# Graph layer kernel: where ScalarE copies a pair's sums out of their bank in the joint part

## The reference

```python
h = jnp.maximum(_layernorm(x, axis=-1), 0.0)             # x: 50000 x 256
S = h[src]                                                # 50000 edges
for r in range(2):                                        # edge type picks the weights
    msgs = where(rel == r, relu(relu(S @ W.T + b) @ W.T + b), msgs)
agg = segment_sum(msgs, dst, num_segments=50000)
i, f, g, o = split(agg @ W_ih.T + b_ih + b_hh, 4)
c = sigmoid(i) * tanh(g);  hn = sigmoid(o) * tanh(c)
y = relu(hn @ W1.T + b1);  y = relu(y @ W2.T + b2)
return x + y @ W3.T + b3
```

## Time and profile before

| | |
|---|---|
| median of 3 runs | 2325.51 us (2324.17 to 2326.1) |
| profiled execution: its time | 2326.91 us |
| profiled execution: span, first to last instruction | 2325.2 us |
| mean granted TensorE clock | 0.958 |
| busy share of PE, PEld, DVE, ACT, POOL | 90, 60, 76, 70, 49% |
| steady joint part | about 604 to 1955 us of the span |

### The profile page before, as it was taken

How to read it: one execution, slowest core, us unless ns; L and a number is a source line. 1 busy time by engine, 2 the same in 40 slices (tenths; PEclk the granted TensorE clock), 3 DMA queues, 4 the chain that set the end, 5 groups by cost and what they waited for, 6 DMA issues and landing times.

```text
span 2325.2 us, 51837 instructions
## 1 busy us (share of the span) xinstructions
PE 2098.4 (90%) x14224; PEld 1403.6 (60%) x14225; DVE 1757.9 (76%) x4311; ACT 1628.3 (70%) x3364; POOL 1150.3 (49%) x917
## 2 busy tenths in 40 slices
PE   6858777657999999999999999999999999999996
PEld 5747565545666666666666666666666666445553
DVE  7537655555788888888888888888888877788886
ACT  2437655546878787877878787878778786666663
POOL 0037777777555565555655556555555543100000
PEclk7559989999999999999999999999999999999998
DMA  9955555557699989989898989998988987998886
GB/s 387 425 180 100 98 98 96 98 93 143 124 175 171 167 170 170 172 171 172 167 172 172 174 166 169 171 172 172 167 172 169 174 156 151 182 193 188 188 188 154
DMA packets 400606, 396.90 MB, mean 171 GB/s; under 512 B 263738, under 2 KB 343158, under 8 KB 394360
## 3 DMA queue, kind: packets, MB, share of 16 engines
q0 software_dynamic: 91200, 157.34, 42.6%
q1 hardware_dynamic: 306788, 238.12, 40.0%
q10 hardware_dynamic: 2516, 0.14, 0.1%
HBM read 185.88 MB, written 156.97 MB: 147 GB/s over the span
## 4 chain that ended last, share of the span: by engine, by line
PE 43%; ACT 25%; issue 16%; POOL 6%; DVE 5%; DMA 4%; another core or an unknown queue 1%; POOLq 0%; SPq 0%; ACTq 0%; DVEq 0%
PE bank L1469 21%; ACT xn L757 4%; PE bank L1452 4%; PE bank L1483 3%; POOL agg L664 3%; PE bank L1416 3%; POOL xg L648 3%; ACT count_tmp L736 3%; ACT row_hi L790 2%; ACT tcell L783 2%; PE bank L1435 2%; PE bank L1508 2%; ACT g_o L777 2%; PE bank L1398 2%; DMA agg<-summed,scatter_idx 2%
## 5 line engine op out<-in xcount | busy, mean ns | idle before, releaser
L664 POOL DMA_INDIRECT agg<-summed,scatter_idx x400 | 638.2, 1596 | 599.7 <-DVE scatter_idx L1144 454.7
L1469 PE MATMUL bank<-a_hi,ihT 128*128 128x512 f16 x2400 | 715.6, 380 | 4.7 <-DMA a_lo<-row_lo 4.7
L648 POOL DMA_INDIRECT xg<-in_x,src_ring x400 | 416.1, 1040 | 270.2 <-DMA src_ring<-src_slot 137.3
L1469 PE MATMUL bank<-a_lo,ihT 128*128 128x512 f16 x1200 | 455.8, 380 | 0.0
L1469 PEld LDWEIGHTS bank<-a_hi,ihT 128*128 128x128 f16 x2400 | 235.0, 98 | 215.7 <-issue 7.2
L1435 PE MATMUL bank<-relT,h_hi 128*128 x1600 | 322.2, 276 | 0.0
L1416 PE MATMUL bank<-s_hi,relT 128*128 128x256 f16 x1600 | 294.8, 280 | 0.0
L672 POOL DMA_DIRECT2D y<-in_x x100 | 133.2, 1341 | 295.2 <-DVE y L1202 284.3
L777 ACT ACTIVATE g_i<-bank,gate_b 128x512 f32<-128x512 f32 x200 | 137.4, 687 | 138.7 <-PE bank L1469 133.3
L1416 PE MATMUL bank<-s_lo,relT 128*128 128x256 f16 x800 | 223.3, 279 | 0.0
L757 ACT ACTIVATE xn<-xg,shift,rstd 128x256 f32<-128x256 f32 x400 | 216.3, 591 | 9.3 <-DVE shift L1111 9.3
(11 more groups left out here) (197 smaller groups left out, 4647.7 us busy)
## 6 DMA issues: line engine op xcount, KB each, us to landing
agg_in<-agg SPq DMA_DIRECT2D x100, 512.0 KB
y<-in_x POOLq DMA_DIRECT2D x100, 512.0 KB, 6.5
out<-y SPq DMA_DIRECT2D x100, 512.0 KB
agg<-zeros SPq DMA_DIRECT2D x24, 2112.0 KB, 15.9
dst_ring<-dst_rows SPq DMA_DIRECT2D x200, 128.0 KB
xg<-in_x,src_ring POOLq DMA_INDIRECT x400
agg<-summed,scatter_idx POOLq DMA_INDIRECT x400
src_ring<-src_slot SPq DMA_DIRECT2D x200, 1.0 KB
```

Source lines behind the costliest of these rows:

```text
L648: nc.gpsimd.indirect_dma_start(out=xg[:, k.slot(8), t, :], out_offset=None, in_=x[:, :], in_offset=bass.IndirectOffsetOnAxis(ap=src_ring[: ...
L664: nc.gpsimd.indirect_dma_start(out=agg[:, :], out_offset=bass.IndirectOffsetOnAxis(ap=scatter_idx[:, k.slot(8), t:t + 1], axis=0), in_=sum ...
L1469: last = nc.tensor.matmul(N_C[c % 2][:, 0:UNIT], lhs, rhs, start=i == 0, stop=i == len(todo) - 1)
```

## The change

In ACT's `both_step` the call `summed_copy(at - 4)` moves from behind `high_m(at - 2)` to right behind `high_s(at)`. Nothing else changes; the other engines' lists are the same row for row.

```diff
             def both_step(at):
                 k, half = at.unit, at.odd
                 high_s(at)
+                summed_copy(at - 4)
                 gate(k, 3 * half)
                 gate(k, 3 * half + 1)
                 if half:
@@
                 tanh_cell(k, half)
                 counts(at - 3)
                 high_m(at - 2)
-                summed_copy(at - 4)
                 if half:
                     relu_2(k - 1)
                 else:
```

## The result

The changed kernel takes 2267.73 us (median of 4 runs, 2265.21 to 2269.79), the kernel before 2324.84 beside it (4 runs, 2322.63 to 2326.1). The ratio is 0.9749, with a 95% interval of 0.9728 to 0.977: faster by 57 us, against 54.8 worked out and 2272 forecast.

The account below looks back on a forecast made before the run. PE sets the steady pace, losing time waiting for ACT's copy at the sums. Savings 46.5 + 5.6 + 1.4 + 1.3 = 54.8 us; 2326.91 - 54.8 = 2272.1, median 2270.7, with 1 us allowed: 2272; 8-in-10 range 2265 to 2290.

Parts of the forecast that it names:

- The place and the size of the wait: PE's sums wait for ACT's copy every second half step; bracket plus 0.16 us each, 46.5 us in the steady part.
- the two kinds: Second half steps, plain or behind the roots: 0.52 us lost per plain one, 0.86 behind the roots.
- That nothing takes its place: Steady part: both waits vanish whole, no other condition holds the sums; four half steps go from 40.03 to 38.65 us.
- The cost at the new place: ACT, 0.47 us ahead of the first gate: 0.24 us spare in three of four half steps, 0.41 behind the roots.
- The allowance for the half steps behind the roots: Reload half steps, ACT's idle time used up exactly: 0 taken, bounds 0 and 7 us; 1 us allowed in the sum.
- Steps 54 to 64: Start of the joint part: 5.6 us from steps 60 to 63 plus 1.4 from steps 57 to 59, 7.0 in all.
- what is saved at the sums of steps 57 to 59 is mostly handed back: Three waits, 4.3 us, returned at PE's second edge layer except behind the last; 1.4 us counted, bounds 0 and 4.3.
- The end: Behind step 199's transposes: 1.7 us, being 0.4 of the steady term and 1.3 from the last steps with pairs.
- the node work alone takes as long as before: Stretch of node work alone: a listed sign that it must take as long as before, so no gain there.
- The DMA rival: DMAs set the real pace, about 2320 to 2326 us, chance 0.04; the forecast put their busy share at 0.92, from 0.89.
- The slower rival: Copy's 0.47 us ahead of ACT's gates enters the path in 144 half steps, 68 us against 54.8 saved: 2339, chance 0.03.
- POOL's earlier start as slack alone: POOL's scatter and the gather behind it move up by some 7 us, which only adds slack for the gathers.

Follow-up runs that it names:

- Experiment 2: Against the changed kernel: copy at its new place in second half steps alone, at its old one in first ones; 2274.59 us, ratio 0.9787.
- experiment 3: Against the changed kernel: copy at its new place in first half steps alone, at its old one in second ones; 2341.68 us, ratio 1.0065.
- experiment 8: The changed kernel run again, unaltered, for a second profile; 2269.63 us, ratio 0.9745.
- experiment 5: Against the changed kernel: an extra unused copy of the sums' bank on ACT ahead of the gates, joint part only; 2277.55 us, ratio 0.9783.
- experiment 6: Copy early in first half steps alone, plus POOL's scatter waiting in joint half steps until ACT has done `m_hi`; 2327.39 us, ratio 0.999.
- experiment 7: The changed kernel plus POOL's scatter waiting in joint half steps until ACT has done `m_hi`; 2270.71 us, ratio 0.9764.

## Why the prediction was right

**The place and the size of the wait** were right. The wait of PE for the copy was the only one in the steady part, it was there in second half steps only (experiments 2 and 3), and its true size is the bracket plus 0.16: the two kinds went from 9.858 to 9.336 and from 10.195 to 9.356 us per half step, 0.52 and 0.84, against 0.52 and 0.86. By brackets alone the steady part would have given 35.6 us; it gave 45.5.

**That nothing takes its place** was right: PE is at 200.00 of 200.

**The cost at the new place** was right: 0.22 and 0.40 us of room are left where 0.24 and 0.41 were worked out. The allowance for the half steps behind the roots was 1 us; they took 0.7 in the first profile of the changed kernel (33 x 0.02), 0.1 in the second.

**Steps 54 to 64** gave 6.0 of 7.0. That what is saved at the sums of steps 57 to 59 is mostly handed back is borne out by PE's wait for `m_lo` ahead of the second edge layer, which grew from 4.8 to 8.8 us; 2.6 of this growth lies in steps 57 to 59, the rest in step 56, ahead of any saving.

**The end** was mis-sized: 1.7 expected behind step 199's transposes, 7.2 seen. The steps that still have pairs gave just the 1.7 (the last sums start 34.35 us behind step 199's transposes before, 32.63 after). The step of the prediction that failed is that the node work alone takes as long as before: it took 346.0 us before and 340.4 after. Most of these 5.5 us are a shorter wait for a transposed tile and the lower granted clock that followed it in the kernel before and not in the changed one (experiment 8). The second profile of the changed kernel has 345.1, by another wait and another clock, so the 5.5 are in good part luck of one execution. Whether the change shortens this stretch can't be told from these. It may: the longest wait for a tile is 1.6 to 2.2 us in the three profiles in which the copy is early everywhere and the scatters are free (the changed kernel twice, experiment 5), and 3.1 to 4.4 in the other seven. Why is not shown.

**The DMA rival** is out: in the stretch from 1200 to 1400 us the share of the DMA engines fell from 0.89 to 0.85 while the rate rose from 170 to 173 GB/s; over the whole steady part it fell from 0.90 to 0.88 while the rate rose from 168 to 175. 0.92 was worked out. So the busy share did not scale with the traffic here; the bound from it was right in its verdict and wrong as a number. This agrees with what the Trainium skill, page "Perfetto Trace Analysis", section "Identifying the Most-Contended Engine", says of that share.

**The slower rival** had the wrong mechanism. Time ahead of the gates does not come onto PE's path one to one: 0.47 us more in each half step cost 5.7 us in the steady part (experiment 5), not 0.47 each time. A kernel that moves the copy and gets slower does exist (experiment 3), but by POOL's timing. The forecast counted POOL's earlier start as slack alone.

## What to carry to other kernels

Where the busiest engine waits for a buffer that another engine empties at the end of its step, look for the first point of that step at which the data is there: an instruction that waits anyway for something later in the same producer's order is such a point, and an idle gap behind it takes the move for free. Size the wait from the distance between neighbouring starts, not from the bracket, where passes are pipelined. And before moving what releases another engine's work, look at which signals that work will then coincide with, and whether they have slack.

## What the runs showed of the hardware that was not expected

Signals from PE to ACT can arrive late while POOL issues indirect DMAs. In the kernel before, ACT's starts that ended a wait for PE came 0.04 us behind the modelled end of the pass, 0.14 at most. In the changed kernel, with a gather begun about 0.37 us before the end of the transposes, ACT's next start came some 1.0 us behind that end, again and again (the half steps from 1169.57 and 1208.21 among them). In experiment 3 it was 1.00 us for `m_hi`, with a scatter begun 0.08 us behind the pass, and 0.49 for the relu, with that scatter still in issue. Counted over the steady part, ACT's starts over 0.15 us late are

| kernel | late, of waits for PE | latest |
|---|---|---|
| before | 0 of 242 | 0.14 us |
| changed, two profiles | 42 of 301, 45 of 310 | 1.09, 1.39 us |
| experiment 3 | 74 of 324 | 1.19 us |
| experiment 6 (3 with the hold) | 3 of 289 | 0.19 us |
| experiment 7 (changed, with the hold) | 6 of 261 | 0.74 us |

Experiment 2 has them too, 29 of its 38 at `h_hi`. Holding the scatters back, and with them the gathers behind, took nearly all of them away, so POOL's timing is shown to be the cause. Which part of an indirect DMA's issue does it, and why other signals in the same kernel pass unhurt, was not tried and is open. So is whether only the signal is late or the end of the pass itself: the ends of passes are modelled, and PE's next passes start on time in both half steps named.
